# A decoder's attention steps: turns of keys and heads moved in the step, inverse norms of queries and keys made apart

## What is computed

```python
qkv = x @ Wqkv; q, k, v = split(qkv)             # 128 -> 3 x 1024
q = l2norm(q) * qs; k = l2norm(k) * ksc          # over the 64 features of a head
q = q*cos*scale + rotate_half(q)*sin*scale       # rotary, k with 1/scale
sim = einsum(q, [k of window before, own window]) * 8   # windows of 32 tokens, masked
x = x + (softmax(sim) @ v) @ Wo
xn = (x - mean) / sqrt(var + 1e-5) * g + bln
a, gate = split(xn @ W1 + b1); x = x + (a * gelu(gate)) @ W2 + b2
```

## Time and profile before

| | us |
|---|---|
| median of 3 runs (2228.61 to 2232.08) | 2229.53 |
| the profiled execution's own time | 2231.51 |
| span of that execution | 2229.7 |
| TensorE matmul busy | 2018.6 (91%) |
| TensorE weight load busy | 1196.2 (54%) |
| VectorE busy | 1360.2 (61%) |
| ScalarE busy | 1361.2 (61%) |
| GpSimd busy | 1079.6 (48%) |

### The profile page before, as it was taken

One profiled execution on the slowest core, in us unless ns is written; L12 is line 12 of the kernel. 1 busy time (PEld: TensorE's weight loads), 2 busy tenths in 40 slices (PEclk: granted clock), 3 DMA queues, 4 the chain that ended last, 5 costly groups with the idle time before them and its releaser, 6 DMA issues.

```text
span 2229.7 us, 73531 instructions
## 1 busy us (share of the span) xinstructions
PE 2018.6 (91%) x32616; PEld 1196.2 (54%) x32616; DVE 1360.2 (61%) x1663; ACT 1361.2 (61%) x1672; POOL 1079.6 (48%) x708
## 2 busy tenths in 40 slices
PE   7999998688999998999999999999899999999987
PEld 4655655355555555555555555555555555555552
DVE  1444444666666766666667666666666666667662
ACT  5555554355666666656666666666666666666664
POOL 0000000476555555555556555655565555555640
PEclk9999998799999999999999999999999999999998
DMA  3000000122223222232222322222232223222220
GB/s 105 1 1 1 1 20 29 29 68 59 59 59 87 68 68 59 59 87 67 70 59 60 83 62 76 74 55 69 76 77 68 60 57 89 68 68 59 59 59 19
DMA packets 81911, 128.02 MB, mean 57 GB/s; under 512 B 17214, under 2 KB 28092, under 8 KB 81468
## 3 DMA queue, kind: packets, MB, share of 16 engines
q1 hardware_dynamic: 81596, 123.33, 21.3%
HBM read 21.55 MB, written 1.05 MB: 10 GB/s over the span
## 4 chain that ended last, share of the span: by engine, by line
PE 64%; ACT 16%; issue 9%; DVE 7%; POOL 4%; POOLq 0%; SPq 0%; DMA 0%; ACTq 0%; DVEq 0%
PE ps L599 14%; PE ps L625 7%; PE ps L603 7%; PE ps L663 5%; PE ps L680 5%; PE ps L656 5%; PE ps L415 4%; ACT KT L977 4%; PE ps L643 3%; PE ps L608 2%; POOL work L1392 2%; DVE work L1070 2%; PE ps L612 2%; DVE work L1067 2%; ACT ps L968 2%
## 5 line engine op out<-in xcount | busy, mean ns | idle before, releaser
L1392 POOL TENSOR_TENSOR work<-work,RS 128x1024 f32<-128x1024 f32 x192 | 361.6, 1904 | 309.9 <-ACT RS L1011 309.9
L603 PEld LDWEIGHTS ps<-ident,work 128*128 128x128 f32 x3072 | 343.6, 142 | 150.5 <-issue 73.5
L1067 DVE TENSOR_TENSOR work<-ps,work 128x1024 f32<-128x1024 f32 x192 | 230.9, 1203 | 311.6 <-ACT work L990 301.3
L603 PE MATMUL ps<-ident,work 128*128 128x128 f32 x3072 | 392.9, 276 | 28.1 <-ACT work L964 12.0
L1386 POOL TENSOR_TENSOR work<-work 128x1024 f32<-128x1024 f32 x96 | 226.2, 2357 | 371.3 <-DVE work L1070 371.3
L599 PE MATMUL ps<-WK,XS 128*128 128x512 f32 x384 | 188.8, 614 | 50.9 <-ACT KT L977 50.8
L1070 DVE TENSOR_TENSOR work<-ps,work 128x1024 f32<-128x1024 f32 x192 | 233.2, 1215 | 0.0
L1106 DVE TENSOR_REDUCE SS<-work 128x16 f32<-128x1024 f32 x192 | 232.1, 1209 | 0.0
L1379 POOL TENSOR_TENSOR work<-work 128x1024 f32<-128x1024 f32 x96 | 226.3, 2357 | 4.3 <-DVE work L1070 4.3
L937 ACT ACTIVATE work<-ps 128x1024 f32<-128x1024 f32 x96 | 98.1, 1022 | 209.2 <-PE ps L663 207.3
L663 PEld LDWEIGHTS ps<-work 64*32 64x32 f32 x12288 | 135.8, 106 | 163.2 <-issue 106.4
(11 more groups left out here) (183 smaller groups left out, 3071.3 us busy)
## 6 DMA issues: line engine op xcount, KB each, us to landing
work<-work SPq DMA_DIRECT2D x576, 128.0 KB
work<-work SPq DMA_DIRECT2D x336, 64.0 KB
WQ<-in_wqkv SPq DMA_DIRECT2D x6, 512.0 KB, 3.7
WK<-in_wqkv SPq DMA_DIRECT2D x6, 512.0 KB, 4.4
WV<-in_wqkv SPq DMA_DIRECT2D x6, 512.0 KB, 3.7
WO<-in_wo SPq DMA_DIRECT2D x6, 512.0 KB, 3.8
work<-ZR SPq DMA_DIRECT2D x48, 64.0 KB
W<-in_w SPq DMA_DIRECT2D x6, 341.0 KB, 2.9
```

What stands on the lines that cost most here:

```text
L603: m = nc.tensor.transpose(flat(R)[:, t * 128:t * 128 + 128], src[:, t * 128:t * 128 + 128], ident[:, :])
L1067: V.tensor_tensor(h16(cos_part[:, j, :]), h16(flat(src)), rotary_tabs[:, at:at + 64].unsqueeze(1).broadcast_to([PARTS, 16, 64]), ALU.mult) ...
L1392: U.tensor_tensor(h16(qk_norm[:, j, :]), h16(cos_part[:, j, :]), inv_norms[:, j, :].unsqueeze(2).broadcast_to([PARTS, 16, 64]), ALU.mult). ...
```

## The change

Nothing in the arithmetic of a result changes but the order, and the norm's scale is multiplied in ahead of its bias in two instructions of VectorE instead of one on ScalarE.
- TensorE: the turn of the heads goes ahead of the values' projection, the turn of the keys goes behind the values' projection and ahead of the work on bank_f; the queries' turn and the keys' projection stay where they were. In n = 1 the second hidden chunk is done whole behind the scores, the gate of the third (behind a wait for the second gelu) between the two halves of the weighing, its value part behind them.
- ScalarE: the copy of the turned heads goes ahead of the copy of the values; the inverse norms are made in two calls, `invert_norms(g, 0)` for the queries (n = 1: between the copy of the turned keys and the load of the gelu table; else ahead of the square of the keys) and `invert_norms(g, 1)` for the keys at the step's end. `copy_heads` stands in n = 1 behind the last gelu and ahead of the table load, in the other steps behind `invert_norms(g, 1)`. The affine is gone. The square of the centred x goes behind the copy of the turned queries.
- VectorE: each sum of squares has its own clamp (16 columns) behind it; the norm has a second instruction for its bias; in n = 1 the second gated product goes behind the shift of the scores.
- GpSimd: the product of the queries goes ahead of the addition for the keys.

```diff
 # TensorE, step
+                if d:
+                    pe.wait_ge(heads_copied, g - 2)
+                    turn(bank_y, heads).then_inc(heads_turned, 1)
                 if b:   # values' projection
...
-                if d:
-                    pe.wait_ge(heads_copied, g - 2)
-                    turn(bank_y, heads).then_inc(heads_turned, 1)
+                if b:
+                    pe.wait_ge(k_normed, g)
+                    if d:
+                        pe.wait_ge(heads_turned_copied, g - 2)
+                    turn(bank_y, qk_norm[:, 1, :]).then_inc(k_turned, 1)
...   # work on bank_f, then the queries' turn
                     pe.wait_ge(hidden_gated, 3 * f + 1)
-                    hid_gate(1, bank_f)
+                    hid(1, bank_f)
...   # first half of the weighing
-                    hid_value(1, bank_f)
+                    pe.wait_ge(gate_gelu, 3 * f + 2)
+                    hid_gate(2, bank_f)
...   # second half of the weighing
                     pe.wait_ge(hidden_gated, 3 * f + 2)
-                    hid(2, bank_f)
+                    hid_value(2, bank_f)
 # ScalarE
+            def invert_norms(g, j):
+                act.wait_ge(sums_clamped, 2 * g + 1 + j)
+                A(norm_logs[:, 16 * j:16 * j + 16], sq_clamped[:, 16 * j:16 * j + 16], ACT.Ln).then_inc(norms_log, 1)
+                act.wait_ge(norms_log, 2 * g + 1 + j)
+                if due(g):
+                    act.wait_ge((q_normed, k_normed)[j], g)
+                A(inv_norms[:, j, :], norm_logs[:, 16 * j:16 * j + 16], ACT.Exp, scale=-0.5).then_inc(inverse_norms, 1)
...   # behind the copy of the turned keys
+                if f is not None and n == 1:
+                    if a:
+                        invert_norms(g, 0)
+                    nc.scalar.preload_act_table_set(GELU)
...   # behind the copy of the turned queries
                 if f is not None and n == 1:
                     gelu(f, 0, bank_f)
+                elif a:
+                    invert_norms(g, 0)
...   # the step's end
-                if c:
-                    copy_heads(g)
                 if f is not None and n == 1:
                     gelu(f, 2, bank_f)
+                    copy_heads(g)
                     nc.scalar.preload_act_table_set(LNEXP)
+                    if a:
+                        invert_norms(g, 1)
+                else:
+                    if a:
+                        invert_norms(g, 1)
+                    if c:
+                        copy_heads(g)
 # VectorE
-                V.tensor_tensor(normed[:, :], bank_f[:, 1, :], spread[:, :], ALU.mult).then_inc(ffn_normed, 1)
+                V.scalar_tensor_tensor(out=normed[:, :], in0=bank_f[:, 1, :], scalar=layer_vecs[...], in1=spread[:, :], op0=ALU.mult, op1=ALU.mult).then_inc(ffn_normed, 1)
+                dve.wait_ge(ffn_normed, f + 1)
+                V.tensor_scalar(ffn_in[:, :], normed[:, :], layer_vecs[...], None, ALU.add).then_inc(ffn_input, 1)
...   # in sums, behind the reduction
+                V.tensor_scalar(sq_clamped[:, 16 * j:16 * j + 16], sq_sums[:, j, :], 1e-24, None, ALU.max).then_inc(sums_clamped, 1)
 # GpSimd
+                    norm_product(g, 0, q_turned, q_rotated, q_normed)
                     pool.wait_ge(k_cos, g + 1)
                     pool.wait_ge(k_sin, g + 1)
                     U.tensor_tensor(cos_part[:, 1, :], cos_part[:, 1, :], sin_part[:, 1, :], ALU.add).then_inc(k_rotated, 1)
+                    norm_product(g, 1, k_turned, k_rotated, k_normed)
```

More of the change, by code:

```diff
@@ L695, in step @@
                 if b:
[L696 to L699, removed]
                     if a:
@@ L945, in step @@
                     A(probs[:, :, :, :], scores_sb[:, :, :, :], ACT.Exp).then_inc(probs_exp, 1)
-                if f is not None and n == 1:
-                    ffn_affine(f)
                 if a:
@@ L965, in step @@
                 if b:
+                    act.wait_ge(values_ready, g)
+                    if due(g - 1):
+                        act.wait_ge(windows_loaded, 160 * (g - 1))
+                    A(v_rows[:, (n - 1) % 2, :], flat(bank_x), ACT.Copy).then_inc(values_copied, 1)
+                if b:
                     act.wait_ge(values_copied, g)
@@ L968, in step @@
                     A(bank_x.rearrange('p q (c k) -> p (q c) k', k=64), seed.unsqueeze(1).broadcast_to([PARTS, 16, 64]), ACT.Copy).then_inc(mask_seeded, 1)
[L969 to L972, removed]
                 if b:
@@ L983, in step @@
                         A(k_t[:, :, 0:32], k_t[:, :, 256:288], ACT.Copy).then_inc(keys_carried, 1)
+                if f is not None and n == 0:
+                    square(f)
                 if f is not None and n == 1:
                     gelu(f, 0, bank_f)
+                elif a:
+                    invert_norms(g, 0)
                 if a:
@@ L1104, in sums @@
                 if due(g):
-                    dve.wait_ge(sums_clamped, g)
+                    dve.wait_ge(sums_clamped, 2 * g - 1 + j)
                 V.tensor_reduce(sq_sums[:, j, :], h16(squares[:, j, :]), AX, ALU.add).then_inc(done, 1)
+                dve.wait_ge(done, g + 1)
+                if due(g):
+                    dve.wait_ge(norms_log, 2 * g - 1 + j)
+                V.tensor_scalar(sq_clamped[:, 16 * j:16 * j + 16], sq_sums[:, j, :], 1e-24, None, ALU.max).then_inc(sums_clamped, 1)
             def step(g, n, a, b, c, d, f, fo):
@@ L1133, in step @@
                     rotary(g, n, 1, bank_y, k_cos, k_sin, k_rotated)
-                if f is not None and n == 1:
-                    gated(f, 1, bank_f)
                 if b:
@@ L1142, in step @@
                     V.tensor_tensor(scores_sb[:, :, :, :], by_head(bank_x), per_head(row_max[:, :]).unsqueeze(3).broadcast_to([PARTS, 8, 2, 64]), ALU.subtract).then_inc(scores_shifted, 1)
+                if f is not None and n == 1:
+                    gated(f, 1, bank_f)
                 if a:
                     sums(1, k_squared, k_sums, g)
-                    dve.wait_ge(q_sums, g + 1)
-                    dve.wait_ge(k_sums, g + 1)
-                    if due(g):
-                        dve.wait_ge(norms_log, g)
-                    V.tensor_scalar(sq_clamped[:, :], sq_sums[:, :, :].rearrange('p a b -> p (a b)'), 1e-24, None, ALU.max).then_inc(sums_clamped, 1)
                 if f is not None and n == 0:
@@ L1368, in scale_tables, with norm_product @@
                 U.tensor_tensor(t, rotary_base[:, :, :, :], qk_scales[:, :, layer, :].unsqueeze(2).broadcast_to([PARTS, 4, 4, 64]), ALU.mult).then_inc(tables_scaled, 1)
+            def norm_product(g, j, turned, rotated, normed_):
+                pool.wait_ge(inverse_norms, 2 * g + 1 + j)
+                pool.wait_ge(rotated, g + 1)
+                if due(g):
+                    pool.wait_ge(turned, g)
+                U.tensor_tensor(h16(qk_norm[:, j, :]), h16(cos_part[:, j, :]), inv_norms[:, j, :].unsqueeze(2).broadcast_to([PARTS, 16, 64]), ALU.mult).then_inc(normed_, 1)
             def step(g, n, a, b, c, d, f, fo):
@@ L1386, in step @@
                     U.tensor_tensor(cos_part[:, 1, :], cos_part[:, 1, :], sin_part[:, 1, :], ALU.add).then_inc(k_rotated, 1)
-                    for j, (turned, rotated, normed_) in enumerate(((q_turned, q_rotated, q_normed), (k_turned, k_rotated, k_normed))):
-                        pool.wait_ge(inverse_norms, g + 1)
-                        pool.wait_ge(rotated, g + 1)
-                        if due(g):
-                            pool.wait_ge(turned, g)
-                        U.tensor_tensor(h16(qk_norm[:, j, :]), h16(cos_part[:, j, :]), inv_norms[:, j, :].unsqueeze(2).broadcast_to([PARTS, 16, 64]), ALU.mult).then_inc(normed_, 1)
+                    norm_product(g, 1, k_turned, k_rotated, k_normed)
             def attention():
```

23 lines of the change are left out of this document (4 added, 19 removed).

## The result

| | us | ratio to before, 95% interval |
|---|---|---|
| before, median of 4 | 2230.8 | |
| after the change, median of 4 (2285.9 to 2296.2) | 2288.5 | 1.0266 [1.0243, 1.0288] |
| the profiled execution after, the slowest of the four | 2296.2 | |

A forecast was written before the change was run, and what follows sets the result against it. TensorE, 91% busy, was taken as the bound. Terms of -0.95, +0.1, -0.25, +1.9 and +1.5 gave +2.3 us a pass, +50.6 over 22; together +52 on 2231.5, 2283.5, so 2282 predicted; range 2248 to 2306.

The forecast's parts named there:

- What is removed: TensorE's waits for the keys' copy and the gated product go; about 3 us a pass if nothing else comes late.
- First place: ScalarE's heads' copy behind the keys' norms, steps 0, 1, 3: changes of +0.1, -0.95 and -0.25 us.
- the mark: Fixed point in TensorE's timeline: the end of the keys' projection, which is the first score.
- Second place: Step 2: the keys' turn waits 2.0 us for ScalarE's copy of the turned heads; +1.9 us.
- Third place: Step 1: clamp held up by GpSimd's addition, then table load; scores wait 2.2 us for the queries' copy; +1.5 us.
- Step 2: From the mark to the step's end: 8.92 us before, less 0.78, plus 2.2 and 0.16, put at 10.45.
- Rival C: The 2 us gaps on TensorE also cost clock, one in three of 44 at 1.5 us: +22, 2304 us; chance 0.13.
- the likeliest: The main forecast, all three places coming late as summed: 2270 to 2294 us; chance 0.51.
- a pass: Four steps, one batch of one layer, 72.4 us before; 22 have both projections and feed-forward work in all steps.
- the steps ahead of the passes: The eight steps before the 22 passes: late keys, a gain of 1.2 and small gains, together +2.5 us.

The follow-up runs named there:

- r2: The changed kernel with the feed-forward output product put back ahead of the keys' turn in step 2 on TensorE; 2263.2 us, ratio 1.0143.
- r4: The changed kernel with the weighed heads' copy ahead of the last gelu in step 1 on ScalarE; 2272.5 us, ratio 1.0187.
- r1: The changed kernel with both clamps as tensor_reduce instead of tensor_scalar; 2262.3 us, ratio 1.0135.
- r10: r7 with the mask seed behind the copy of the turned keys on ScalarE; 2182.5 us, ratio 0.9777.
- r7: r6 with a sixth edit: second gated product ahead of the scores' maximum in step 1 on VectorE; 2182.9 us, ratio 0.9795.
- r3: The changed kernel with the turned queries' copy ahead of the queries' norms and gelu table load in step 1; 2245.6 us, ratio 1.0070.
- r8: The changed kernel with the value windows' copies issued behind the block's scores on SyncE; 2287.8 us, ratio 1.0263.
- r6: The changed kernel with r1, r2, r3, r4 and the heads' copy ahead of the keys' norms in the other steps; 2188.2 us, ratio 0.9824.
- r9: r7 with value windows copied for the first two blocks only, so the output differs; 2167.1 us, ratio 0.9708.

## Why the prediction was right

Forecast 2282, measured 2288.5; +52 us forecast, +57.7 measured. The mechanism was the one forecast, at all three places. That the number is so near is in part luck: some terms were too large and one was missing. Step by step, in the prediction's own order:
- What is removed: right. The two waits are gone, to 9.4 and to nothing.
- First place: right in sign and near in size. The chain from the mark to the clamp's end is 7.24 us (1015.76 to 1023.00) against 7.31. The steps came out at 16.95 (17.1), 16.6 (16.5) and 17.7 (18.0). The wait of the heads' turn was forecast at 0.9 us in every step 0 and 1. It is 0.5 us and comes 13 times in 21 passes; the steps came out right even so, because the copy of the turned heads further down sets them.
- Second place: right. The keys' turn waited 1.82 us (2.0), in all 22 passes; from the step's start to the mark 12.65 us (12.9). r2 and r4 show that it is the place in the order against ScalarE's queue, from both sides.
- Third place: right. The scores waited 2.17 us (2.2), of which 1.2 are the clamp (r1). Counted from the mark at 1015.76, the second rotary product ended at 13.64 (13.8), the clamp at 16.19 (16.35), and the scores started at 19.12 (19.3). The norm's second instruction took 2.07 us, which I had not priced by itself; the row sum started 0.3 us behind the end of the exponential, the delay that I had allowed for it. The terms of my sum for this place add up to 10.50 and not to 10.45, and the 0.78 in it stands there without its working.
- Step 2, from the mark to its end, took 11.84 us in the pass shown where I had 10.45. The missing 1.39 is a stop within the scores (1038.41). I had left the stops called issue as they were, 24 us for the two lines; after the change they are 37. In other passes a lower clock adds about as much. The whole of step 2 takes 22.7 to 23.1 us in the 6 of 21 passes that are short, against 23.35 forecast, and 24.0 or more in the other 15. So my terms were some 0.5 too large, and the term for stops and clock, which I had put at nothing, was missing.
- Rival C, with 0.13, came true in part beside the likeliest: the gap of 2.17 us cost clock in 11 of the 22 passes (below).
- Over 21 passes (568.84 to 2112.36 before, 577.65 to 2177.59 after, first scores of a step 1) a pass grew by 2.7 us where I had 2.3. By steps, in the mean: step 1 -1.15 (-0.95), step 2 +3.86 (+3.4), step 3 -0.22 (-0.25), step 0 +0.22 (+0.1). For 22 passes that makes 59 instead of 50.6. The stretch up to the first mark (568.84 before; 575.48 after, the score's start less its wait) grew by 6.6 us, where I had 2.5 for the steps ahead of the passes.
- The profiled execution lies 7.7 us above the median here, and I had taken off 2.0. Profiled against profiled, the forecast 2283.5 was 12.7 too low; a part of the distance is hidden by the choice of execution.

## What to carry to other kernels

Read from the trace not only how long a queue's owner is busy, but when in the step the instruction that others wait for comes out of its queue: a consumer moved ahead of the work that covered it (here 2.6 us of matmuls) stalls by the difference, even if the producer didn't get slower. Before adding a `tensor_scalar` on VectorE that reads and writes SBUF, look whether GpSimd is at work at that moment: the same operation as a reduction cost 0.19 us where the tensor_scalar cost 1.4. And when a wait of TensorE ahead of bursts of small matmuls is removed, read the stops within them again: in the profiled execution of r10 they had grown by more than the wait had shrunk.

## What was not expected of the hardware

**A tensor_scalar waits for GpSimd's instruction to end, short or long.** The 512-column `tensor_scalar` of the norm takes 485 ns alone and 2066 in the median of the source view, in all 22 passes until 0.27 to 0.29 us behind the end of GpSimd's product that it met; the 16-column one ends 0.04 behind. The reductions and the products with one operand in PSUM, beside the same GpSimd instructions, keep their 1.21 us. Nor is it enough to be small and to read SBUF: in the kernel before, 95 of the 96 reciprocals of 16 columns (L1117) lie wholly inside a GpSimd instruction, and none took over 0.26 us. This agrees with what the Trainium skill, "SBUF — State Buffer", section "SBUF: two separate sides", says of the exclusive lock, for both sizes: the instruction that starts first has the shared ports for its whole length, and the other waits.

**The clock.** In the pass at 1111 us the scores also started 2.17 us late, and then:

```profile
1111.54 1.05 PE L656 MATMUL ps<-KT,work 64*32 64x64 f32 x64 [2.17 <-issue]
1112.52 1.97 PE L603 MATMUL ps<-ident,work 128*128 128x128 f32 x8
1114.41 1.22 PE L656 MATMUL ps<-KT,work 64*32 64x64 f32 x64
```

The 8 turns took 1.97 us instead of 1.09 and the 64 scores 1.22 instead of 0.86. The windows view of that stretch (busy us by engine, then granted clock, DMA share, GB/s) has the clock:

```profile
1105.00:1110.00 5.00, 4.37 (x17) 2.05 (x15) 3.57 (x3) 3.29 (x6) 4.40 (x5) 1.00 0.53 130
1110.00:1115.00 5.00, 3.46 (x112) 2.99 (x114) 2.79 (x3) 3.40 (x5) 1.26 (x1) 0.67 0.31 83
```

The granted clock of those 5 us is 0.67: about 3.3 of them at 1.2 GHz and the rest at 2.4. Ahead of it TensorE had run 8 us without a stop (1101.12 to 1109.37) and then idled for 2.17. From 560 to 2160 us the kernel after the change spent some 41 us at the lower level in 12 such places, the kernel before 7, r1 (wait 0.96) and r7 (no such wait) 3 and 0, r2, which keeps the wait of 2.17 and drops the one of 1.82, 44. So it is mostly the wait ahead of the scores: 11 of the 12 places stand right behind it. The twelfth stands behind the wait of 1.82 in step 2 (1277.87), behind which come long matmuls, and there is none in r3, which has that wait 22 times and the other not at all. How many of the 22 waits of about 2.2 us cost clock differs from kernel to kernel: 11 here, 12 in r2, 7 in r8. What decides it, no run here tells.

One such place costs 1.2 us (1111.54 to 1115.56 is 4.02; the same stretch of the pass above is 2.79 without its stop). Twelve are some 15 of the 23.1 us by which TensorE's busy time grew, and most of what r3 saved beside its waits. The executions after the change spread over 10 us, with mean granted clocks of 0.974 for 2296.2 us and 0.981 for 2285.9; but r6, without that wait, spreads as far (2185.8 to 2195.7), so these places are not shown to be the reason.

**Stops in bursts of small matmuls.** TensorE stops by 0.3 to 1.6 us at places some 38 us apart, in the 64-column matmuls (L656, L663), before the change and after. Many lie at the same matmul of the program in different kernels: with 44, 43 and 19 matmuls left of the burst at 645, 687 and 719 us in the kernel before, and at 647, 691 and 722 in r3. They last 0.4 to 0.8 us before, 0.8 to 1.2 there. r3 has one more, of 0.84 us at 687 with 39 left, where the kernel before has none. Their place in the program points to the supply of instructions, which no run here tests; without the window copies (r9) they add up to 25.8 us instead of 42.1. What sets the rest, and why they are shorter in the kernel before, stays open.
